# Sequence layer with sparse side path and ternary feed-forward: last head pair and feed-forward part as one instruction program

## The chip, the cores and the metric

The kernel runs on one core of a Trainium2 chip. The metric is the device time of one execution in microseconds; a lower number is better. Times of a timeline are counted from the first instruction of the profiled execution. PE is TensorE, DVE is VectorE, ACT is ScalarE, POOL is GpSimd, SP is SyncE, which here only issues DMAs.

## The reference

One layer over 1024 tokens of width 256, all in fp32. The attention is multi-head with 16 heads, compressed queries and keys (layer-normed), rotary position parts, a causal softmax, and a small side path over 8 selected tokens, which adds one row per head. What the change touches is the second half:

```python
def ternary_quant(w):
    scale = jnp.mean(jnp.abs(w)) + EPS
    q = jnp.clip(jnp.round(w / scale), -1.0, 1.0) * scale
    return w + jax.lax.stop_gradient(q - w)

x = layernorm(x + attention(x))                 # x: (1, 1024, 256)
up   = x @ ternary_quant(W_up).T                # W_up, W_gate: (1024, 256)
gate = x @ ternary_quant(W_gate).T
y = (silu(up) * gate) @ ternary_quant(W_down).T # W_down: (256, 1024)
out = layernorm(x + y)
```

## The kernel before

**Steps and slots.** The heads are worked on in 8 pairs. A list of steps (`PROLOGUE`, `FIRST`, `MID` in a loop, `LAST`, `EPILOGUE`) is written out by hand, and each engine runs the part of each step that belongs to it, in the order of the list. So a step's place in the list is its place in the queue of every engine that takes part in it. A head has 8 slots, one per tile of 128 queries. In slot i: `qk` (five matmuls per chunk of 512 keys into `SC[i % 2]`, line 618 on), DVE's mask with maximum (L1006), ACT's exp (L845) into `Pb[i % 2]`, then `tc`: PE transposes the probabilities (L636), ACT copies them out rounded (`PTh`, L832), DVE subtracts to get the rest (`PTl`, L943). Every fp32 operand goes through PE as such a pair of high and low parts (fp32r). `pv` (L610 to L612) multiplies with the values for 256 queries at a time, `wo` multiplies with the output weights and adds into `acc` (L1143). The last chunks of a head (`tc` of tile 7, `wo` 2, `pv` 3, `wo` 3) stand in the first slots of the next one. The four single PSUM banks `J` go round over all steps that use one; the two double banks `SC` belong to `qk`.

**The last pair** (heads 14 and 15, `LAST`) has no next pair to prepare; the steps of `mlp_steps` (line 277) are in its slots instead. `wld` loads the three weight matrices of the feed-forward part (1 MB each) into `kvraw`, `KX` and `QX`, `wabs` (ACT, L866) sums absolute values, `wtot` turns them into scale and thresholds (a small matmul, and five tiny DVE operations), `tern` makes the ternary values of 512 columns with two DVE operations (L1080: is it below the negative threshold; L1082: is it above the positive one, minus the first), twelve times, in place. `wt` transposes 512 columns of the result on PE (L771) and ACT copies them into `xTh`, `xTl` (up, gate) and `KNh`, `KNl` (down), twelve times. `rowadd` adds the side path's row (L1132), `ln1` and `ln1n` are the layer norm for 256 tokens, `ht` transposes their normed values (L775) and splits them.

**The feed-forward part** is a second block, `mlp` (from line 1165), which starts when all engines have ended the first. It norms and transposes tokens 512 to 1023 itself. Its unit is 512 tokens times 128 hidden columns, 16 of them: `up_gate` (8 matmuls of 512 columns, L1241, L1242), the sigmoid (ACT, L1288), two products (DVE `tt` L1344, `hid` L1349), the rounded copy (ACT `Hh`, L1276), the rest (POOL `Hl`, L1218), and three units later `down` (8 matmuls of 256 columns, L1253, L1254), which accumulates over 8 units in the four banks `J`. After units 7 and 15: residual for four token tiles (L1312), statistics (L1318), POOL's power of -0.5, the norm (L1329), and the store. The second accumulation waits for the first four residuals.

```python
pe.wait_ge(hl_done, n + 1)
if n == ET:
    pe.wait_ge(y_done, 4)
```

## Time and profile before

| what | us |
|---|---|
| median of 3 runs | 739.39 (738.97 to 739.4) |
| the profiled execution, its own time | 743.51 |
| its span, first to last instruction | 741.7 |
| PE busy | 670.4 (90%) |
| DVE busy | 490.9 (66%) |
| ACT busy | 397.5 (54%) |
| POOL busy | 338.9 (46%) |

The page gives busy times over the whole span. A share there is a mean over parts with different limits, so the stretches around the change have to be read apart: the windows give busy time per engine between two moments, and the timeline gives each instruction with, in brackets, the idle time of its engine ahead of it and what ended that. Head 14 begins with its first mask at 600.60, head 15 at 633.78; the first matmul of the feed-forward block is at 682.17.

### The profile page before, as it was taken

The page shows a single profiled execution, that of the slowest core. Times are in us where ns is not written, and L with a number is a line of the kernel's source. Part 1 is how long each engine was busy: PE and PEld are TensorE (multiplying, and loading weights), DVE is VectorE, ACT ScalarE, POOL GpSimd, SP SyncE. Part 2 cuts the span into 40 slices and gives each one's busy share as a digit, 9 for nine tenths or more (in the row PEclk, how much of TensorE's full clock was granted, in tenths as well). Part 3 has the DMA queues.
Part 4 walks back from the last instruction along what each step waited for, and adds up shares of the span by engine and source line. Part 5 has one row for each costly group of instructions (what it writes and reads, how often), then busy time and mean ns, then how long its engine had stood idle before and what let it go on. Part 6 is the DMA issues. An engine that isn't in the chain of part 4 may idle for free. (4 is left out here: it accounts for less than half of the span.)

```text
span 741.7 us, 14057 instructions
## 1 busy us (share of the span) xinstructions
PE 670.4 (90%) x4416; PEld 600.9 (81%) x4416; DVE 490.9 (66%) x1401; ACT 397.5 (54%) x920; POOL 338.9 (46%) x279
## 2 busy tenths in 40 slices
PE   5667799999999999999999999999999999878994
PEld 5546699889988898899889988998899889767883
DVE  2665366666676666666766676667666668996665
ACT  3341345764576457645764476447644766644531
POOL 5622354735474547354735474547454730000443
PEclk9965599999999999999999999999999999998998
DMA  6153210551045105510541055105410545000001
GB/s 200 44 141 72 64 50 1 124 112 51 1 103 134 50 0 120 113 50 0 125 108 50 0 127 106 50 0 129 104 50 0 127 86 171 1 0 1 1 1 57
DMA packets 29486, 50.50 MB, mean 68 GB/s; under 512 B 8976, under 2 KB 20496, under 8 KB 29456
## 3 DMA queue, kind: packets, MB, share of 16 engines
q1 hardware_dynamic: 29456, 50.12, 27.0%
q8 instruction: 16, 0.26, 0.1%
q14 instruction: 14, 0.11, 0.1%
HBM read 15.50 MB, written 1.05 MB: 22 GB/s over the span
## 5 line engine op out<-in xcount | busy, mean ns | idle before, releaser
L943 DVE TENSOR_TENSOR PTl<-J,PTh 128x512 fp32r<-128x512 f32 (+1 forms) x192 | 102.2, 553 | 65.3 <-ACT PTh L832 64.7
L845 ACT ACTIVATE Pb<-SC,nm 128x128 f32<-128x128 f32 (+7 forms) x128 | 94.8, 740 | 62.9 <-DVE nm L1010 62.9
L1006 DVE CUSTOM_DVE_ANT_0 SC<-SC,mask 128x128 f32<-128x128 f32 (+7 forms) x128 | 97.3, 760 | 28.0 <-PE SC L627 25.8
L610 PE MATMUL J<-PTh,Vh 128*128 128x256 f32 x320 | 88.3, 276 | 7.0 <-DVE PTl L943 6.8
L636 PE MATMUL J<-ident,Pb 128*128 128x128 f32 x576 | 88.1, 279 | 6.0 <-ACT Pb L845 5.5
L612 PE MATMUL J<-PTh,Vl 128*128 128x256 f32 x320 | 89.3, 279 | 0.0
L611 PE MATMUL J<-PTl,Vh 128*128 128x256 f32 x320 | 89.3, 279 | 0.0
L832 ACT ACTIVATE PTh<-J 128x512 fp32r<-128x512 f32 (+1 forms) x192 | 87.5, 493 | 2.6 <-PE J L636 1.7
L636 PEld LDWEIGHTS J<-ident,Pb 128*128 128x128 f32 x576 | 63.8, 141 | 13.8 <-ACT Pb L845 5.4
L610 PEld LDWEIGHTS J<-PTh,Vh 128*128 128x128 f32 x320 | 60.7, 190 | 11.7 <-DVE PTl L943 10.4
L623 PE MATMUL SC<-KNh,QNh 128*128 128x512 f32 (+1 forms) x192 | 69.0, 360 | 0.0
L624 PE MATMUL SC<-KNl,QNh 128*128 128x512 f32 (+1 forms) x192 | 66.8, 348 | 0.0
L625 PE MATMUL SC<-KNh,QNl 128*128 128x512 f32 (+1 forms) x192 | 66.8, 348 | 0.0
L626 PE MATMUL SC<-KD,QS 128*128 128x512 f32 (+1 forms) x192 | 66.7, 347 | 0.0
L627 PE MATMUL SC<-KL,QS 128*128 128x512 f32 (+1 forms) x192 | 66.6, 347 | 0.0
L832 ACT ACTIVATE ATh<-J 128x256 fp32r<-128x256 f32 x64 | 24.5, 383 | 69.6 <-PE J L612 68.9
L611 PEld LDWEIGHTS J<-PTl,Vh 128*128 128x128 f32 x320 | 60.6, 189 | 0.7
L612 PEld LDWEIGHTS J<-PTh,Vl 128*128 128x128 f32 x320 | 60.9, 190 | 0.0
L1143 DVE SCALAR_TENSOR_TENSOR acc<-J,rs,acc 128x256 f32<-128x256 f32 x128 | 56.1, 480 | 2.6
L943 DVE TENSOR_TENSOR ATl<-J,ATh 128x256 fp32r<-128x256 f32 x64 | 27.0, 422 | 45.1 <-ACT ATh L832 45.0
L907 ACT ACTIVATE kvraw<-kvraw,nmr,rstd 128x128 f32<-128x128 f32 x128 | 52.5, 485 | 5.0 <-POOL nmr L589 5.0
L832 ACT ACTIVATE kvraw<-J 128x512 f32<-128x512 f32 x32 | 19.2, 599 | 65.8 <-PE J L612 65.8
(283 smaller groups left out, 1869.9 us busy)
## 6 DMA issues: line engine op xcount, KB each, us to landing
KD<-RKh SPq DMA_DIRECT2D x32, 256.0 KB, 4.5
KL<-RKl SPq DMA_DIRECT2D x32, 256.0 KB, 5.0
KX<-KX SPq DMA_DIRECT2D x16, 256.0 KB, 2.4
QX<-QX SPq DMA_DIRECT2D x16, 256.0 KB, 2.3
QS<-RQh SPq DMA_DIRECT2D x16, 256.0 KB, 4.0
QS<-RQl SPq DMA_DIRECT2D x16, 256.0 KB, 4.5
r_kv<-in_L_attn_W_ckv SPq DMA_DIRECT2D x8, 384.0 KB, 3.4
r_qn<-in_L_attn_W_qT SPq DMA_DIRECT2D x16, 128.0 KB, 2.8
```

The costliest lines, as they stand in the source:

```text
L610: mm(o, lhsT=wh, rhs=xh, start=start, stop=False)
L611: mm(o, lhsT=wh, rhs=xl, start=False, stop=False)
L612: return mm(o, lhsT=wl, rhs=xh, start=False, stop=stop)
L623: mm(o[:, k], lhsT=QNh[b][:, q], rhs=KNh[b][:, k], start=True, stop=False)
L624: mm(o[:, k], lhsT=QNh[b][:, q], rhs=KNl[b][:, k], start=False, stop=False)
L625: mm(o[:, k], lhsT=QNl[b][:, q], rhs=KNh[b][:, k], start=False, stop=False)
L626: mm(o[:, k], lhsT=QS[b][:, q], rhs=KD[b][:, k], start=False, stop=False)
L636: last = pe.transpose(o[:, tile(j - 4 * c)], Pb[i % 2][:, tile(j)], ident[:, :])
L832: return act.activation(o, i, ACT.Copy)
L845: act.activation(Pb[i % 2][:, w], SC[i % 2][:, w], ACT.Exp, bias=nm[:, i % 2:i % 2 + 1], scale=SCALE, accum_out=sm[:, b, i:i + 1]).then_in ...
L943: dve.tensor_tensor(o, i, h.bitcast(F32), ALU.subtract).then_inc(done[kind], 1)
L1006: dve.tensor_tensor_reduce(out=SC[i % 2][:, w], in0=SC[i % 2][:, w], in1=mask[:, 128 * (7 - i):S], scale=1.0, scalar=LOW, op0=ALU.add, op1 ...
```

## The change

- The host hands over the three feed-forward weights transposed. The twelve `wt` steps are gone; `tern` writes its result straight to where the matmuls read it.
- The first operation of `tern`, the compare, moves from DVE to POOL. DVE waits for it, and POOL waits for the combine two pieces back.
- Two of the three weights are loaded at the start of head 14 (ahead of the transfers `stk` and `stq` in SP's queue), the third in slot 3. Sums, scales and eight of the twelve `tern` steps lie in head 14, four in head 15; the row additions move from slots 3 and 4 of head 15 to 0 and 1.
- The second block is gone. Its work becomes steps of the list: `ug` (up and gate), `m` (sigmoid, products, copy, rest), `dn` (down), `h2` (late transposes), `res`, `ost`, `onorm`. They stand in `EPILOGUE`, mixed with the last chunks of head 15 and the layer norms of the later tokens. The buffers lie in memory that the attention no longer needs.
- The unit is 256 tokens times 128 hidden columns, 32 of them. Four halves of `SC` banks hold four units, `down` comes five units later, and two accumulators of `J` alternate with the other two.

```diff
                 if b == 0:
-                    add(2, True, ("wld", 0, 0))
-                    add(4, True, ("wld", 0, 1), ("wabs", 0, 0))
-                    add(5, True, ("wabs", 0, 1))
-                    add(6, True, ("wtot", 0, 0), ("wld", 0, 2), ("tern", 0, 0), ("wabs", 0, 2))
-                    add(7, True, ("tern", 0, 1), ("wabs", 0, 3))
+                    add(0, True, ("wld", 0, 0), ("wld", 0, 1))
+                    add(1, True, ("wabs", 0, 0))
+                    add(2, True, ("wabs", 0, 1))
+                    add(3, True, ("wtot", 0, 0), ("wld", 0, 2), ("wabs", 0, 2))
+                    add(4, True, ("wabs", 0, 3), ("tern", 0, 0), ("tern", 0, 1))
+                    add(5, True, ("wtot", 0, 1), ("tern", 0, 2), ("tern", 0, 3))
+                    add(6, True, ("tern", 0, 4), ("tern", 0, 5), ("wabs", 0, 4))
+                    add(7, True, ("tern", 0, 6), ("tern", 0, 7), ("wabs", 0, 5))
                 else:
-                    add(0, True, ("wtot", 0, 1), ("tern", 0, 2))
-                    add(1, True, ("tern", 0, 3), ("wabs", 0, 4))
-                    add(2, True, ("wt", 0, 0), ("tern", 0, 4), ("wabs", 0, 5))
-                    add(3, True, ("rowadd", 0, 0), ("rowadd", 0, 1), ("wt", 0, 1), ("wt", 0, 2), ("tern", 0, 5), ("tern", 0, 6))
-                    add(4, True, ("wtot", 0, 2), ("wt", 0, 3), ("tern", 0, 7), ("rowadd", 0, 2), ("rowadd", 0, 3))
-                    add(5, True, ("wt", 0, 4), ("tern", 0, 8), ("ln1", 0, 0))
-                    add(6, True, ("wt", 0, 5), ("tern", 0, 9), ("ln1n", 0, 0), ("ln1", 0, 1))
-                    add(7, True, ("wt", 0, 6), ("wt", 0, 7), ("tern", 0, 10), ("tern", 0, 11), ("ln1n", 0, 1))
+                    add(0, True, ("wtot", 0, 2), ("rowadd", 0, 0), ("rowadd", 0, 1))
+                    add(1, True, ("rowadd", 0, 2), ("rowadd", 0, 3), ("tern", 0, 8))
+                    add(2, True, ("tern", 0, 9))
+                    add(3, True, ("tern", 0, 10))
+                    add(4, True, ("tern", 0, 11))
+                    add(5, True, ("ln1", 0, 0))
+                    add(6, True, ("ln1n", 0, 0), ("ln1", 0, 1))
+                    add(7, True, ("ht", 0, 0), ("ln1n", 0, 1))
...
-        EPILOGUE = [*t(NH - 1, 7), ("ht", 0, 0), ("wo", NH - 1, 2), ("wt", 0, 8), ("wt", 0, 9), ("pv", NH - 1, 3),
-                    ("ht", 0, 1), ("wt", 0, 10), ("wt", 0, 11), ("wo", NH - 1, 3)]
+        def one(kind, n):
+            return (kind, 0, n)
+
+        def mlp_steps_of(n):
+
+            a = [one("ug", n), one("m", n - 2)]
+            q, e = divmod(n - LAG, ET)
+            if n >= LAG:
+                a.append(one("dn", n - LAG))
+            a += {7: [one("h2", 2)], 9: [one("h2", 3)]}.get(n, [])
+            if q >= 1:
+                a += {1: [one("res", q - 1)], 2: [one("ost", q - 1)], 4: [one("onorm", q - 1)]}.get(e, [])
+            return a
+
+        EPILOGUE = [one("ug", 0), one("ug", 1), *t(NH - 1, 7), ("wo", NH - 1, 2), one("ht", 1), ("pv", NH - 1, 3), one("m", 0),
+                    one("ln1", 2), one("ug", 2), one("ug", 3), one("m", 1), ("wo", NH - 1, 3), one("ln1n", 2), one("ug", 4),
+                    one("m", 2), one("ln1", 3), one("ug", 5), one("m", 3), one("dn", 0), one("ug", 6), one("ln1n", 3),
+                    one("m", 4), one("dn", 1)]
+        for n in range(7, NM):
+            EPILOGUE += mlp_steps_of(n)
...
+        EPILOGUE += [one("m", NM - 2), one("onorm", 2), one("m", NM - 1)] + [one("dn", n) for n in range(NM - LAG, NM)]
+        EPILOGUE += [one("res", 3), one("ost", 3), one("onorm", 3)]
 
...
                     if kind == "wld":
-                        src = (W_up, W_gate, W_down)[c]
-                        if c == 0:
+                        src = (W_upT, W_gateT, W_downT)[c].rearrange("(k p) n -> p k n", p=128)
+                        if c == 2:
                             sp.wait_ge(ready["kt"], PER["kt"] * NH)
                             sp.wait_ge(done["vs"], NH)
                         else:
-                            sp.wait_ge((rk_ready, rq_ready)[c - 1], NP)
-                        sp.dma_start(raw[c], src.rearrange("(t p) d -> p t d", p=128)).then_inc(ld_mlp[c], 16)
+                            sp.wait_ge((rk_ready, rq_ready)[c], NP)
+                        sp.dma_start(raw[c].rearrange("p (k n) -> p k n", n=src.shape[2]), src).then_inc(ld_mlp[c], 16)
+                    if kind == "onorm":
+                        sp.wait_ge(y_ln, c + 1)
+                        sp.dma_start(out[256 * c:256 * c + 256, :].rearrange("(t p) d -> p t d", p=128),
+                                     yo[:, 2 * c:2 * c + 2, :]).then_inc(stored, 16)
...
+                    if kind == "tern":
+                        w, j = c // 4, c % 4
+                        if j == 0:
+                            gp.wait_ge(thr_ready, w + 1)
+                        wait(gp, tern_done, c - 1)
+                        gp.tensor_scalar(low[c % 2], raw[w][:, half(j)], nthr[:, w:w + 1], None, ALU.is_lt).then_inc(low_done, 1)
+                    if kind == "m":
+                        gp.wait_ge(hh_done, c + 1)
+                        gp.tensor_tensor(Hl[c % HB], hid[c % 4], Hh[c % HB].bitcast(F32), ALU.subtract).then_inc(hl_done, 1)
+                    if kind == "ost":
+                        q = slice(2 * c, 2 * c + 2)
+                        inv_std(mv2[:, q, 1], ve2[:, q], rsd2[:, q], y_ag, c + 1, y_ve, y_rsd, c + 1)
...
+            def up_gate(n):
+                wait(pe, hid_done, n - 3)
+                if n % ET == 0:
+                    if n < 2 * ET:
+                        pe.wait_ge(done["ht"], n // ET + 1)
+                    else:
+                        pe.wait_ge(done["h2"], n // ET - 1)
+                if n == 0:
+                    pe.wait_ge(tern_done, 8)
+                if n % 4 < 2 and n < 4:
+                    pe.wait_ge(exp_done, T * NH - 1)
+                elif n < 4:
+                    pe.wait_ge(exp_done, T * NH)
+                tok = slice(256 * (n // ET), 256 * (n // ET) + 256)
+                o = SC[n % 4 // 2]
+                for w in range(2):
+                    z = slice(512 * (n % 2) + 256 * w, 512 * (n % 2) + 256 * w + 256)
+                    for k in range(K):
+                        wt = (xTh, xTl)[w][:, k, tile(n % ET)]
+                        mm(o[:, z], lhsT=wt, rhs=hTh[k][:, tok], start=k == 0, stop=False)
+                        last = mm(o[:, z], lhsT=wt, rhs=hTl[k][:, tok], start=False, stop=k == K - 1)
+                last.then_inc(ug_ready, 1)
+
...
+            def down(n):
+                q, e = divmod(n, ET)
+                pe.wait_ge(hl_done, n + 1)
+                if n == 0:
+                    pe.wait_ge(tern_done, 12)
+                    pe.wait_ge(done["wo"], PER["wo"] * NH)
+                if n == ET:
+                    pe.wait_ge(done["h2"], 2)
+                if e == 0 and q >= 2:
+                    pe.wait_ge(y_done, 2 * q - 2)
+                wt = (KNh, KNl)[e // 4][0][:, D * (e % 4):D * (e % 4) + D]
+                for t in range(2):
+                    o = J[2 * (q % 2) + t]
+                    mm(o[:, 0:D], lhsT=Hh[n % HB][:, tile(t)], rhs=wt, start=e == 0, stop=False)
+                    last = mm(o[:, 0:D], lhsT=Hl[n % HB][:, tile(t)], rhs=wt, start=False, stop=e == ET - 1)
+                last.then_inc(dn_ready, 1)
+
+            def late_transposes(c):
+                pe.wait_ge(ln_done, c + 1)
+                pe.wait_ge(done["wo"], PER["wo"] * NH)
+                for m in range(4):
+                    last = pe.transpose(J[c][:, tile(m)], acc[:, 2 * c + m % 2, tile(m // 2)], ident[:, :])
+                last.then_inc(ready["h2"], 1)
+
             def run(steps, p, before):
...
+            def hidden_hi(n):
+                act.wait_ge(hid_done, n + 1)
+                wait(act, dn_ready, n - HB + 1)
+                copy(Hh[n % HB], hid[n % 4]).then_inc(hh_done, 1)
...
+                    if kind == "m":
+                        act.wait_ge(ug_ready, c + 1)
+                        wait(act, tt_done, c - 3)
+                        act.activation(sg[c % 4], up_of(c), ACT.Sigmoid, scale=scl[:, 0:1]).then_inc(sg_done, 1)
+                        if c >= 1:
+                            hidden_hi(c - 1)
+                        if c == NM - 1:
+                            hidden_hi(c)
...
                     if kind == "tern":
                         w, j = c // 4, c % 4
-                        if w == 2:
-                            v, lw = raw[2][:, j // 2, half(j % 2)], low[c % 2]
-                        else:
-                            v, lw = raw[w][:, 2 * j:2 * j + 2, :], low[c % 2].rearrange("p (t d) -> p t d", t=2)
+                        v, lw = raw[w][:, half(j)], low[c % 2]
+                        dst = (xTh, xTl)[w][:, j // 2, half(j % 2)] if w < 2 else (KNh, KNl)[j // 2][0][:, half(j % 2)]
                         if j == 0:
                             dve.wait_ge(thr_ready, w + 1)
-                        if c == 0:
-                            dve.wait_ge(rq_ready, NP)
-                        if c >= 2:
-                            dve.wait_ge(tern_done, c - 1)
-                        dve.tensor_scalar(lw, v, nthr[:, w:w + 1], None, ALU.is_lt).then_inc(low_done, 1)
                         dve.wait_ge(low_done, c + 1)
-                        dve.scalar_tensor_tensor(v, v, thr[:, w:w + 1], lw, ALU.is_gt, ALU.subtract).then_inc(tern_done, 1)
+                        dve.scalar_tensor_tensor(dst, v, thr[:, w:w + 1], lw, ALU.is_gt, ALU.subtract).then_inc(tern_done, 1)
+                    if kind == "m":
+                        dve.wait_ge(sg_done, c + 1)
+                        dve.scalar_tensor_tensor(tt[c % 4], up_of(c), scl[:, 0:1], sg[c % 4], ALU.mult, ALU.mult).then_inc(tt_done, 1)
+                        dve.wait_ge(tt_done, c + 1)
+                        wait(dve, hl_done, c - 3)
+                        dve.scalar_tensor_tensor(hid[c % 4], gate_of(c), scl[:, 1:2], tt[c % 4], ALU.mult, ALU.mult).then_inc(hid_done, 1)
+                    if kind == "res":
+                        dve.wait_ge(dn_ready, ET * (c + 1))
+                        for t in range(2):
+                            dve.scalar_tensor_tensor(yo[:, 2 * c + t, :], J[2 * (c % 2) + t][:, 0:D], scl[:, 2:3], acc[:, 2 * c + t, :],
+                                                     ALU.mult, ALU.add).then_inc(y_done, 1)
+                    if kind == "ost":
+                        for t in range(2 * c, 2 * c + 2):
+                            dve.wait_ge(y_done, t + 1)
+                            dve.bn_stats(st2[:, t, :], yo[:, t, :]).then_inc(y_st, 1)
+                        for t in range(2 * c, 2 * c + 2):
+                            dve.wait_ge(y_st, t + 1)
+                            ins = dve.bn_aggr(mv2[:, t, :], st2[:, t, :])
+                        ins.then_inc(y_ag, 1)
+                    if kind == "onorm":
+                        dve.wait_ge(y_rsd, c + 1)
+                        dve.wait_ge(y_ag, c + 1)
+                        for t in range(2 * c, 2 * c + 2):
+                            ins = dve.tensor_scalar(yo[:, t, :], yo[:, t, :], mv2[:, t, 0:1], rsd2[:, t:t + 1], ALU.subtract,
```

## Rows read from the trace of the kernel before

**Rows 1.** The page: busy time and share by engine, granted TensorE clock by slice.
```profile
PE 670.4 (90%) x4416; PEld 600.9 (81%) x4416; DVE 490.9 (66%) x1401; ACT 397.5 (54%) x920; POOL 338.9 (46%) x279
...
PEclk9965599999999999999999999999999999998998
```

**Rows 2.** Windows: start:end length, busy PE PEld DVE ACT POOL, clock, DMA, GB/s.
```profile
600.60:633.78 33.18, 31.25 (x221) 28.38 (x220) 25.27 (x68) 23.89 (x56) 3.42 (x2) 1.00 0.41 122
601.00:613.00 12.00, 11.18 (x82) 9.93 (x81) 7.87 (x24) 8.54 (x24) 3.42 (x2) 1.00 0.34 68
612.00:633.78 21.78, 20.67 (x143) 18.86 (x142) 18.00 (x46) 15.15 (x33) 0.00 (x0) 1.00 0.43 146
633.78:665.79 32.01, 27.25 (x191) 24.09 (x190) 30.47 (x87) 15.77 (x38) 0.91 (x2) 1.00 0.00 1
665.79:732.86 67.07, 58.70 (x336) 50.77 (x336) 43.77 (x92) 29.46 (x53) 23.93 (x22) 0.95 0.03 9
732.86:741.70 8.84, 0.00 (x0) 0.00 (x0) 4.73 (x16) 0.00 (x0) 1.21 (x2) 0.61 0.17 59
```

**Rows 3.** Timeline of DVE and ACT in heads 14 and 15: start us, us, instruction.
```profile
627.76 0.48 DVE L1080 TENSOR_SCALAR CS<-kvraw,nthr 128x512 f32<-128x512 f32 x1
628.28 0.75 DVE L1082 SCALAR_TENSOR_TENSOR kvraw<-kvraw,thr,CS 128x512 f32<-128x512 f32 x1
...
650.38 0.79 ACT L845 ACTIVATE Pb<-SC,nm 128x640 f32<-128x640 f32 x1 [2.93 <-DVE nm L1010]
...
653.80 1.29 DVE L1132 TENSOR_TENSOR acc<-acc,row 128x512 f32<-128x512 f32 x2
```

**Rows 4.** Timeline of PE from the last mask to the second half of the feed-forward part.
```profile
667.66 0.66 PE L771 MATMUL J<-ident,KX 128*128 128x128 f32 x4 [2.00 <-DVE ATl L943]
...
676.79 0.28 PE L610 MATMUL J<-PTh,Vh 128*128 128x256 f32 x1
...
682.17 0.47 PE L1241 MATMUL SC<-QNh,xTh 128*128 128x512 f32 x1 [1.52 <-PEq L1156]
...
715.75 0.36 PE L1253 MATMUL J<-KNh,Hh 128*128 128x256 f32 x1 [1.24 <-DVE yo L1312]
```

**Rows 5.** Windows of 5 us around the hand-over, columns as in rows 2.
```profile
650.00:655.00 5.00, 3.13 (x24) 2.87 (x25) 4.71 (x16) 2.35 (x5) 0.00 (x0) 1.00 0.00 0
665.00:670.00 5.00, 2.41 (x19) 1.72 (x17) 4.17 (x12) 3.23 (x7) 0.89 (x2) 0.99 0.00 0
670.00:675.00 5.00, 4.33 (x21) 4.04 (x20) 4.85 (x12) 2.21 (x5) 0.00 (x0) 0.50 0.02 3
```

**Rows 6.** Timeline of PE in the steady ring of the feed-forward part.
```profile
695.82 0.40 PE L1241 MATMUL SC<-QNh,xTh 128*128 128x512 f32 x1
...
697.64 0.28 PE L1253 MATMUL J<-KNh,Hh 128*128 128x256 f32 x1
...
698.58 0.40 PE L1241 MATMUL SC<-QNh,xTh 128*128 128x512 f32 x1
```

**Rows 7.** Groups by line (busy, mean ns, idle before), one line's instructions, SP's timeline.
```profile
L576 POOL CAST Vh<-kvraw 128x1024 fp32r<-128x1024 f32 x16 | 16.7, 1041 | 80.3 <-ACT kvraw L907 80.3
...
L1218 POOL TENSOR_TENSOR Hl<-hid,Hh 128x512 fp32r<-128x512 f32 x16 | 20.7, 1291 | 24.3 <-ACT Hh L1276 24.3
...
L548 POOL TENSOR_TENSOR Wqnl<-r_qn,Wqnh 128x256 fp32r<-128x256 f32 x16 | 11.8, 737 | 1.3
...
L1143 DVE SCALAR_TENSOR_TENSOR acc<-J,rs,acc x128: 472/480/486, 101.6 to 681.4; 128x256 f32<-128x256 f32 x128
...
L1288 ACT ACT_TABLE_LOAD x1 | 1.3, 1283 | 1.4 <-PEq L1156 1.4
...
588.04 0.46 SPq L426 DMA_DIRECT2D QS<-RQh  x1
```

**Rows 8.** Timeline of DVE after the last matmul.
```profile
732.86 1.66 DVE L1312 SCALAR_TENSOR_TENSOR yo<-J,scl,acc 128x256 f32<-128x256 f32 x4 [3.32 <-PE J L1254]
...
737.64 1.38 DVE L1329 TENSOR_SCALAR yo<-yo,mv,rsd 128x256 f32<-128x256 f32 x4 [1.40 <-POOL rsd L1226]
```

More of the change, by code:

```diff
@@ L41 @@
 NB = 4
+ET = E // 128
+NM = 4 * ET
+LAG = 5
 CHUNKS = [(i + 4) // 4 for i in range(T)]
@@ L145, in attention_and_mlp, with ring, up_of, gate_of @@
         low = [CS[:, 0, 512 * c:512 * c + 512] for c in range(2)]
-        raw = [kvraw[:, :, :], KX[:, :, :].rearrange("p k n -> p (k n)").rearrange("p (t d) -> p t d", t=T), QX[:, :, :]]
+        raw = [X[:, :, :].rearrange("p k n -> p (k n)") for X in (KX, QX, kvraw)]
         junk = CS[:, 1, :]
+        def ring(X, n=4):
+            return [X[:, 256 * i:256 * i + 256] for i in range(n)]
+        HB = 8
+        hTh, hTl = (QNh[0], QNl[0]), (QS[0], KD[0])
+        Hh, Hl = ring(RKh) + ring(RKl), ring(RQh) + ring(RQl)
+        sg, tt, hid = ring(QX[:, 0, :]), ring(QX[:, 1, :]), ring(CS[:, 0, :])
+        yo = KX[:, :, :].rearrange("p k n -> p (k n)").rearrange("p (t d) -> p t d", t=T)
+        def up_of(n):
+            return SC[n % 4 // 2][:, 512 * (n % 2):512 * (n % 2) + 256]
+        def gate_of(n):
+            return SC[n % 4 // 2][:, 512 * (n % 2) + 256:512 * (n % 2) + 512]
+        st2, mv2 = sb("st2", [128, T, 6]), sb("mv2", [128, T, 2])
+        ve2, rsd2 = sb("ve2", [128, T]), sb("rsd2", [128, T])
         mx = sb("mx", [128, 2])
@@ L243, in attention_and_mlp @@
         PER = {"xt": 4, "qc": T, "qm": 4, "kv": 4, "kpe": 2, "qp": 2, "kt": 2, "ab": 1, "qn": 2,
-               "vs": 1, "pv": 4, "wo": 4, "side": 11, "tc": NCH, "wb": 1, "rw": 1, "wtot": 3, "wt": 12, "ht": 2}
+               "vs": 1, "pv": 4, "wo": 4, "side": 11, "tc": NCH, "wb": 1, "rw": 1, "wtot": 3, "ht": 2}
         def count(kind, unit, c):
@@ L496, in _ @@
             run(LAST, NP - 1)
+            run(EPILOGUE, 0)
+            sp.wait_ge(stored, 64)
         LD_C, LD_SIDE, LD_W0 = 16 * 8, 16 * 8, 16 * 7
@@ L762, in use @@
                     last = mm(o[:, 0:2], lhsT=onesf[:, :], rhs=asum[:, 2 * c:2 * c + 2], start=True, stop=True)
-                if kind == "wt":
-                    w, q = c // 4, c % 4
-                    pe.wait_ge(tern_done, 4 * (w + 1))
-                    for m in range(4):
-                        if w < 2:
-                            src = raw[w][:, 4 * (q % 2) + m, tile(q // 2)]
-                        else:
-                            src = raw[w][:, m % 2, tile(2 * q + m // 2)]
-                        last = pe.transpose(o[:, tile(m)], src, ident[:, :])
                 if kind == "ht":
@@ L796, in run @@
                         qk(unit(kind, off, p), p + off // 2, off % 2, c)
+                    elif kind == "ug":
+                        up_gate(c)
+                    elif kind == "dn":
+                        down(c)
+                    elif kind == "h2":
+                        late_transposes(c)
                     elif kind in BANKED_ALL:
@@ L846, in run @@
                                        scale=SCALE, accum_out=sm[:, b, i:i + 1]).then_inc(exp_done, 1)
-                    if kind in ready and kind not in ("side", "wb", "wtot", "wo", "rw"):
+                    if kind in ready and kind not in ("side", "wb", "wtot", "wo", "rw", "h2"):
                         act.wait_ge(ready[kind], count(kind, u, c))
```

227 lines of the change are left out of this document (27 added, 200 removed).

## The prediction

> **What bounds the kernel now.** I read the page first: TensorE (PE) is busy 90% of the span and VectorE (DVE) 66%, and the granted clock is full in most slices, with dips near the end [rows 1]. Then I cut the part that the change touches into stretches [rows 2] and looked for the engine with no idle time in each. Head 14 (the first of the last pair) takes 33.18 us with PE busy for 31.25: PE sets its pace. From the first mask of head 15 at 633.78 to its last one at 665.79 the picture turns round: 32.01 us, DVE busy 30.47, PE only 27.25. The DVE timeline shows why: each ternary piece is a compare (0.48) and a combine (0.75), started 0.51 and 0.67 apart, 1.18 us for the two, and ten of the twelve pieces lie in head 15, with four row additions (0.6 each) [rows 3] and half of the first layer norm. The third stretch, 67.07 us from there to the last matmul at 732.86, has 8.4 us of idle PE. The PE timeline shows where some of it sits: 2.00 us ahead of a weight transpose, 1.52 at the start of the second block (released by a queue, not by data), 1.24 in the middle of the feed-forward part while the residual empties the four accumulators [rows 4]. PE was busy 2.41 us in 665 to 670, and the granted clock was 0.50 in the next five [rows 5]; that is 1.2 GHz. Last comes a tail without any matmul, 8.84 us. In the feed-forward ring itself PE has no gap: eight matmuls of 512 columns take 1.82 us (695.82 to 697.64), eight of 256 take 0.94 (to 698.58) [rows 6].
>
> **The change, stretch 1: the ternary work (600.60 to 665.79, 65.19 us).** Leaves DVE: 12 compares. Moves from head 15 to head 14: combines 2 to 7 and the second set of scale steps (0.7). In head 15, DVE loses eight pieces of 1.18 (2 to 9) and 0.7, and keeps four combines of 0.67 ahead of the last mask: 9.4 + 0.7 - 2.7 = 7.4 us less, which gives a floor of 32.0 - 7.4 = 24.6. PE loses 28 transposes of the weights there (0.11 each, 3.1) and has some 22 us of its own up to that mask. With both engines near 90% neither runs without gaps; head 14, where PE had 31.25 of 33.18 and DVE 25.27, shows gaps of 2 us at that load [rows 2]. I take 26.5, 5.5 less than before. Head 14: DVE gains eight combines (5.4) and one more set of scale steps (0.7) and loses two pieces (2.4), 3.7 us, against 3.8 us idle from 612.00 to 633.78; ScalarE gains two more absolute sums (1.1 each) in slots 1 and 2, against 3.5 us idle from 601.00 to 613.00 [rows 2]. The cover is all used up, so I charge 1.0; the bounds are 0 and +3. Stretch 1 is 4.5 us shorter.
>
> The compares go to GpSimd, which is busy for 3.4 us of head 14 and 0.9 of the rest [rows 2]. None of its rows is a compare with a scalar; the nearest are the cast (1041 ns for 1024 columns, so 0.6 for 512) and the two-input subtraction (1291 for 512) [rows 7]. Either is hidden: two are needed per slot of about 4 us, and DVE's combine of piece c waits for one issued a slot before. If one took over 2 us, DVE would stand behind it with its masks, and ScalarE's exps behind those. GpSimd's compares queue behind nothing but the value split of head 15, its only work in head 14 (3.4 us). Loads: the first two now come earlier, behind the last stacking transfer of head 14 at 588.04 [rows 7], and ahead of head 15's stacking, which is wanted only at 633; the four transfers that follow them on SP wait a few us at most, at no cost. The third is wanted in slot 6. Host-side transposition isn't in the device time.
>
> **Stretch 2: hand-over and feed-forward (665.79 to 732.86, 67.07 us).** PE's work after the change: 256 up/gate matmuls of 256 columns at 0.1175 (30.1; before 128 of 512 at 0.228, 29.1), 128 down matmuls (15.0), 16 transposes of the normed tokens in `ht` and `h2` (1.8), and what is left of head 15: 15 transposes 1.7, `pv` 2.1 and 2.8, `wo` 1.4. Sum 54.9. Now the idle time, counted from the last mask M. DVE's mask 1.4, then exp, `pv`'s eviction, `ht` 0's copies and subtractions: `ug` 0 can start at about M+6.0, while PE's own work ends at M+3.4: idle 2.6. The transposes of tile 7 then `wo`, `ht` 1; `pv` 3 waits 0.6 for its subtraction and ends at M+13.4. ScalarE reaches the first sigmoid only behind `pv` 3's copy, and behind a table load of 1283 ns [rows 7]: M+15.1. From there DVE is the bound: each step `m` is two products. A product of 256 columns with one PSUM input takes 480 ns [rows 7], 0.39 from start to start (four of them in 1.66) [rows 8], so a step costs 0.91, and between the first ones lie `wo` 3 (1.0) and two layer norms (1.6 each). PE waits for the fourth `hid` before: 6.3 us idle in all up to `ug` 10 at M+27.9, the 2.6 and 0.6 included. After that a step costs PE 0.94 + 0.47 = 1.41, DVE 0.91, GpSimd 0.74 (256-column subtraction, 737 ns) [rows 7] and ScalarE 0.7, so PE is the bound again; residual and norm of a quarter cost DVE 2.6 per eight steps against 4.0 spare, and use other accumulators than the next quarter, so the 1.24 us goes. At the end the last `ug`'s chain (sigmoid, two products, copy, subtraction, 3.6 with `onorm` 2 between) outlasts the downs in hand: 1.3 idle, and 0.5 I give to small gaps. 54.9 + 6.3 + 1.3 + 0.5 = 63.0, 4.1 less. So nearly all of this gain is work (2.2 of 20 weight transposes, 3.3 that matmuls lose at half clock, from 670.1 to 676.8, where the 256-column matmul is back at 0.28 [rows 4, 5]), and the idle time moves rather than shrinks. Bounds: 60 (DVE's extra steps overlap better) and 66 (they don't overlap, and the clock falls again).
>
> ScalarE's switch of tables: the row shows 1283 ns, with 1.4 us idle ahead of it put down to the block's start [rows 7]. If that idle is the switch's own, it now stands in the stream, and the first sigmoid comes 1.4 later. The Trainium skill, ScalarE: Activation LUTs, section What ACT_TABLE_LOAD costs, says the switch is a load of about 1283 ns and a drain of about 1380 ns; the row agrees on the load and can't tell for the drain; by that rule the sum would be 1.4 higher.
>
> **Stretch 3: the tail (8.84 us).** Before: four residuals from 732.86, statistics, GpSimd's power, four normalisations from 737.64 [rows 8], and 2.7 from the end of these to the end of the span. Now only two tiles are left: 0.9 + 0.8 + 0.35 for residual, statistics and their sum, 0.1 of hand-over, 0.9 on GpSimd, 0.8 for the norm, 2.7 for the store: 6.6, 2.2 less.
>
> Sum: 4.5 + 4.1 + 2.2 = 10.8 us. The profiled execution took 743.51 with a span of 741.7, so its own time would be 732.7. The median of the runs is 739.39, 4.1 below the profiled one, and the cut is the same: **728.6**.
>
> **The rivals.** (a) The table switch costs the full 2.7 in the stream: 730.0. For: the idle time of just that size; against: every engine waited then. (b) The clock falls once more, as in [rows 5], through PE's wait ahead of `ug` 0; 6.7 us at 1.2 GHz cost 3.3: 731.9. Against: 3.13 busy of five at 650 to 655 left it full, and the new stretch has about that. (c) Head 15 doesn't get shorter, since what sets it is the round mask, exp, transpose, subtraction, `pv`, and DVE was only full beside it: 728.6 + 5.5 = 734.1. For: DVE's load was spread over gaps; against: an exp waited 2.93 us for its mask there [rows 3]. It is also the case where the spreading does nothing. (d) Slower: GpSimd's compares hold up DVE. No compare in the trace ran on GpSimd beside a DVE operation with two SBUF inputs, which the combines and row additions have. If DVE stood still for each compare, 12 x 1.29 = 15.5 us on the stretches where it is the bound: 744.1. It decides from 0.9 us per compare on. Against: the subtraction on GpSimd takes 1291 ns on average beside DVE's products in the ring. The Trainium skill, GPSIMD Engine Reference, section 8. Key points, says that GpSimd shares its SBUF interfaces with VectorE and contends with instructions in a 2-port mode or with two SBUF inputs; no run here shows it yet. (e) Slower too: half clock stays through the feed-forward part, where PE waits for DVE in the first steps. A step then costs 2.8 and not 1.41; eight such steps eat the gain, fourteen give 748.
>
> **How the numbers follow.** Chances: forecast 0.46, (a) 0.14, (b) 0.17, (c) 0.13, (d) 0.06, (e) 0.04. The likeliest is the forecast, 728.6. The range: downward, stretch 1 at its floors (2.9 less) and a fill with 2 us less idle: 724; upward past (c) with a part of (a): 736. (d) and (e) are left out, and with misses at both ends that is about 0.2. A measurement of this kernel tells 0.2% (1.5 us) from no change. Faster 0.89; same 0.04 (half of (d), and chance sums of (b) and (c)); slower 0.07.
>
> **What would show it.** Stretch 1: from head 15's first mask to its last about 26.5 us, DVE busy under 95%; head 14 about 34. Compares on GpSimd of 0.6 to 1.3 us each, combines still 0.75. Stretch 2: 63 us from last mask to last matmul, PE idle ahead of `ug` 0 and from `ug` 4 to `ug` 9, none of over 0.3 after that; first sigmoid 1.7 after the end of `pv` 3. Stretch 3: 6.6. Wrong if combines are longer beside compares, if the granted clock is 0.5 past the hand-over, or if head 15 keeps its 32 us with DVE idle.

## The result, and the profile after

| | before | changed kernel |
|---|---|---|
| median, us (first comparison, 6 runs each) | 739.39 (738.97 to 742.97) | 734.7 (731.98 to 736.2) |
| ratio | | 0.9925 [0.9898, 0.9953] |
| median, us (second comparison, 9 and 5 runs) | 740.83 (739.51 to 742.04) | 734.32 (732.39 to 736.45) |
| ratio | | 0.9905 [0.9889, 0.9921] |
| profiled execution, own time / span, us | 743.51 / 741.7 | 736.02 / 734.2 |

The change makes the kernel faster, by 0.75% and 0.95% (4.7 and 6.5 us). The forecast was 728.6: the sign is right, and 734.7 lies in the range of 724.0 to 736.0, but the forecast gain was 10.8 us, and about half of it came.

The page after the change: busy time by engine, and the granted clock by slice [rows 1].

```profile
PE 667.7 (91%) x4496; PEld 604.6 (82%) x4496; DVE 491.5 (67%) x1421; ACT 397.2 (54%) x940; POOL 365.4 (50%) x313
...
PEclk9875599999999999999999999999999999999998
```

The totals say little: nearly the same work, with POOL busy 26.5 us longer. The windows of the stretches of [rows 2] tell more. First head 14, from its first mask; then head 15 to its last mask; the hand-over and the feed-forward part up to the last residual pair; the tail; and three windows of 5 us at the hand-over, which answer [rows 5]. The columns are length, busy PE, PEld, DVE, ACT, POOL, clock, DMA share and GB/s.

```profile
601.18:637.10 35.92, 32.67 (x224) 28.76 (x223) 28.44 (x78) 25.99 (x60) 17.08 (x10) 1.00 0.26 65
637.10:662.43 25.33, 22.35 (x154) 20.14 (x152) 23.85 (x70) 9.80 (x26) 9.05 (x6) 1.00 0.00 1
662.43:727.99 65.56, 57.55 (x453) 55.31 (x452) 50.35 (x127) 33.43 (x81) 29.10 (x44) 0.97 0.04 13
727.99:734.20 6.21, 0.00 (x0) 0.00 (x0) 2.49 (x8) 0.00 (x0) 0.89 (x2) 0.59 0.13 42
...
660.00:665.00 5.00, 3.86 (x32) 3.54 (x30) 4.72 (x13) 2.11 (x5) 0.89 (x2) 1.00 0.00 0
665.00:670.00 5.00, 3.08 (x17) 3.08 (x18) 1.95 (x5) 1.08 (x5) 0.00 (x0) 0.77 0.00 0
670.00:675.00 5.00, 4.65 (x35) 4.44 (x34) 2.90 (x7) 1.85 (x4) 0.00 (x0) 0.89 0.01 3
```

| stretch | before | forecast | after |
|---|---|---|---|
| head 14 | 33.18 | 34.2 | 35.92 |
| head 15 to its last mask | 32.01 | 26.5 | 25.33 |
| last mask to last matmul | 67.07 | 63.0 | 65.56 |
| tail | 8.84 | 6.6 | 6.21 |
| sum from the start of head 14 | 141.1 | 130.3 | 133.0 |

Head 15 gave more than forecast, head 14 cost more, and the stretch at the hand-over kept most of what it was to lose. Its 65.56 us hold 57.55 of PE busy and 8.0 of PE idle. The idle time is the 8.1 that the forecast had (2.6, 3.7 more in the first steps, 1.3 and 0.5); the busy time is 2.6 above the 54.9. The clock column shows a part of it: 0.77, then 0.89. PE's timeline shows the waits and the slower matmuls.

```profile
666.92 0.39 PE L867 MATMUL SC<-QNh,xTh 128*128 128x256 f32 x1 [3.06 <-DVE KD L1238]
667.14 0.28 PE L868 MATMUL SC<-QS,xTh 128*128 128x256 f32 x1
...
668.39 0.41 PE L868 MATMUL SC<-QS,xTh 128*128 128x256 f32 x1
668.61 0.41 PE L867 MATMUL SC<-QNl,xTh 128*128 128x256 f32 x1
...
679.38 0.39 PE L867 MATMUL SC<-QNh,xTh 128*128 128x256 f32 x1 [0.64 <-DVE CS L1197]
681.21 0.38 PE L867 MATMUL SC<-QNh,xTh 128*128 128x256 f32 x1 [0.62 <-DVE CS L1197]
683.86 0.39 PE L867 MATMUL SC<-QNh,xTh 128*128 128x256 f32 x1 [0.78 <-DVE CS L1197]
688.16 0.39 PE L867 MATMUL SC<-QNh,xTh 128*128 128x256 f32 x1 [0.33 <-DVE CS L1197]
...
727.21 0.39 PE L884 MATMUL J<-KNl,RKl 128*128 128x256 f32 x1 [1.90 <-POOL RQl L641]
```

The first `ug` waits 3.06 us for the subtraction of `ht` 0 (L1238), as forecast. Less than a microsecond later the matmuls of 256 columns follow each other every 0.21 us instead of 0.12, which is the lower level, 1.2 GHz. Then `ug` waits for DVE's second product (L1197) four times, 2.4 us in all, and never again by over 0.3. At the end the last `down` waits 1.90 us for GpSimd.

Two later runs, `e2_short_sums` and `e7_short_combines`, have this same stretch with no edit in it, and in both the clock stays full. Here is the stretch in `e2_short_sums`, and the 5 us up to where the clock fell in the changed kernel with the 3.4 us after it:

```profile
661.19:725.35 64.16, 55.99 (x453) 53.76 (x452) 50.36 (x128) 33.32 (x81) 29.11 (x44) 1.00 0.04 14
...
661.46:666.46 5.00, 1.93 (x17) 1.70 (x16) 4.05 (x10) 3.08 (x7) 0.88 (x2) 1.00 0.00 0
666.46:669.86 3.40, 3.40 (x30) 3.18 (x28) 0.91 (x2) 1.09 (x2) 0.00 (x0) 1.00 0.00 0
```

and the last two in the changed kernel:

```profile
662.70:667.70 5.00, 1.94 (x17) 1.70 (x16) 4.05 (x10) 3.08 (x7) 0.88 (x2) 1.00 0.00 0
667.70:671.10 3.40, 3.40 (x18) 3.40 (x17) 0.00 (x0) 0.12 (x1) 0.00 (x0) 0.50 0.00 0
```

The engines had done the same in both up to that moment, PE after a wait of 3.07 and 3.06 us. Then one execution kept the full clock and the other had half of it for 3.4 us. The low level cost the stretch 1.4 us (65.56 against 64.16; 64.18 in `e7_short_combines`). Of the five profiled executions with this order, three had it (also `e1_compare_dve` and `e9_after_again`) and two had not.

### The profile page after: what moved, and what is told of

The parts are those of the page before. It is cut to its first block, busy times and chain, and to the rows that moved or that the text cites. A ratio compares the mean times of both kernels' runs of the same rounds, so it can differ in the third digit from the quotient of the medians.

```text
span 734.2 us, 14324 instructions
## 1 busy us (share of the span) xinstructions
PE 667.7 (91%) x4496; PEld 604.6 (82%) x4496; DVE 491.5 (67%) x1421; ACT 397.2 (54%) x940; POOL 365.4 (50%) x313
## 3 DMA queue, kind: packets, MB, share of 16 engines
HBM read 15.50 MB, written 1.05 MB: 23 GB/s over the span
## 4 chain that ended last, share of the span: by engine, by line
PE 57%; DVE 16%; ACT 11%; issue 9%; POOL 4%; SPq 1%; DMA 0%; ACTq 0%; DVEq 0%; POOLq 0%
PE J L676 10%; PE J L678 9%; PE J L677 9%; DVE PTl L1059 4%; PE J L702 4%; ACT kvraw L1023 3%; PE SC L693 3%; PE SC L690 3%; PE SC L691 3%; PE SC L692 3%; ACT Pb L960 3%; PE SC L689 3%; POOL rstd L608 3%; DVE SC L1122 3%; ACT PTh L942 2%
## 5 line engine op out<-in xcount | busy, mean ns | idle before, releaser
L630 POOL CAST Vh<-kvraw 128x1024 fp32r<-128x1024 f32 x16 | 16.6, 1037 | 81.0 <-ACT kvraw L1023 81.0
```

## The experiments

Each edit is against the changed kernel. Stretches are those of the table.

**The compares back on DVE** (`e1_compare_dve`).

```diff
 # GpSimd
-if kind == "tern": ...
-    gp.tensor_scalar(low[c % 2], raw[w][:, half(j)], nthr[:, w:w + 1], None, ALU.is_lt)...
 # DVE, ahead of the combine
+wait(dve, tern_done, c - 1)
+dve.tensor_scalar(lw, v, nthr[:, w:w + 1], None, ALU.is_lt).then_inc(low_done, 1)
```

> The changed kernel with the 12 compares of the ternary work back on DVE, nothing else. Theory (the move to GpSimd is what shortens DVE's queue): DVE gets 12 x 0.51 = 6.1 us more in a stretch where it is busy 22 of 24.5 us (head 14 from its fourth mask) and 23.9 of 25.3 (head 15), so head 14 goes from 35.9 to about 38 and head 15 up to its last mask from 25.3 to about 27.3; 4 to 5 us longer than the changed kernel, ratio to the kernel before about 0.999. Rival (DVE and GpSimd hinder each other, since the compares take 1.6 to 2.6 us on GpSimd and one combine beside one took 1.10 in place of 0.74): the move bought little, both heads within 0.5 us of the changed kernel, ratio about 0.993.

Measured: 742.51 us, 1.0022 [1.0001, 1.0042] of before. Its windows for head 14 and for head 15:

```profile
601.49:641.60 40.11, 33.94 (x226) 29.87 (x225) 32.35 (x86) 26.16 (x60) 3.41 (x2) 0.98 0.22 58
641.60:669.49 27.89, 24.23 (x155) 21.58 (x155) 25.27 (x75) 9.80 (x26) 0.91 (x2) 0.91 0.00 1
```

With the compares on DVE, stretch 1 is 68.0 us against 61.25, and longer than before (65.19). So the spreading over both heads alone brings nothing; the move to GpSimd is worth 6.8 us, more than the 4 to 5 expected. Eight compares of 0.51 are 4.1 of the 4.2 us by which head 14 grew: each of its last four slots holds two compares and is 1.04 to 1.05 us longer, the first three of them ahead of any low clock. In head 15 four compares are 2.0 of 2.6, and there the clock is also lower (0.91). DVE's idle time in head 14 covers none of these compares.

**The absolute sums over 8 columns** (`e2_short_sums`).

```diff
-src, o = raw[w][:, S * j:S * j + S], junk
+src, o = raw[w][:, S * j:S * j + 8], junk[:, 0:8]
```

> The changed kernel, but each of the six absolute sums on ScalarE reads 8 columns, not 1024, so its scale is of 8 columns only (work left out). Theory (head 14 took 2.7 us longer because two more sums stand in ScalarE's queue in slots 1 to 4, ahead of copies and exps that PE waits for): each sum falls from 1.15 us to 0.3 and head 14 from 35.9 to 33.5 to 34. Rival (it is DVE's eight combines and scale steps): head 14 stays at 35.3 or more.

Measured: head 14 35.09 us, 0.83 shorter; head 15 the same (25.35); 733.37 us in one run. That lies between the theory (33.5 to 34) and the rival (35.3 or more). ScalarE's busy time in head 14 is 21.36 us instead of 25.99: 4.6 us less of its work give 0.8, so most of the growth is not ScalarE's. Single profiles can carry such a difference: in five executions with the changed kernel's head 14 and a full clock it took 35.82 to 35.96 us.

**The first part alone** (`e3_pair_only`): the changed last pair, then the old second block.

```diff
-EPILOGUE = [one("ug", 0), one("ug", 1), *t(NH - 1, 7), ...]   # ug, m, dn, h2, res, ost, onorm
+EPILOGUE = [*t(NH - 1, 7), ("wo", NH - 1, 2), ("ht", 0, 1), ("pv", NH - 1, 3), ("wo", NH - 1, 3)]
...
+mlp(nc, top, SC, J, acc, ident, mhalf, epst, ...)   # as before, 512 tokens at a time
```

> First part of the change alone: weights from the host in transposed form, ternary work spread and shared as in the changed kernel, but the feed-forward part as in the kernel before (own block, 512 tokens at a time). If the parts add up as the windows say, the last pair gives 3.9 us up to the last mask, the 20 weight transposes behind it 2.2, and the clock falls or not as PE idles there (0 to 3): 5 to 8 us less than before in the profile, and the second part is then worth about nothing in its long stretch and 2.6 in the tail: ratio 0.990 to 0.994. Rival (the second part carries most of the gain, by the block boundary and the tail): ratio above 0.996.

Measured: 735.63 us, 0.9933 [0.9903, 0.9963]. Its windows from the last mask to the first matmul of the block, and from there to the last residuals:

```profile
659.88:672.68 12.80, 7.76 (x62) 6.83 (x61) 8.60 (x24) 5.17 (x13) 0.89 (x2) 1.00 0.00 0
672.68:723.33 50.65, 48.09 (x264) 41.21 (x264) 32.88 (x64) 21.82 (x37) 23.07 (x20) 0.97 0.03 12
```

The first part gives nearly the whole gain. Without the weight transposes, and with the clock full where it was 0.50 before [rows 5], the hand-over takes 12.80 us (16.38 before); the block takes 50.65 (50.69 before). One program with units of 256 tokens is then 2.1 us longer (65.56 against 63.45) in this stretch and 2.7 shorter in the tail (6.21 against 8.87), in the profiles from head 14 on 0.4 us shorter in sum (133.0 against 133.4). Both profiles hold 3.4 us of low clock in this stretch.

**Tile 7 ahead of the first two up/gate groups** (`e4_tile7_first`).

```diff
-EPILOGUE = [one("ug", 0), one("ug", 1), *t(NH - 1, 7), ("wo", NH - 1, 2), one("ht", 1), ...
+EPILOGUE = [*t(NH - 1, 7), ("wo", NH - 1, 2), one("ug", 0), one("ug", 1), one("ht", 1), ...
```

> The changed kernel with the transposes of the last query tile and wo 2 ahead of the first two ug steps in the list (they stand behind them in the changed kernel). Theory (the 3.06 us in which PE waits for the split of the normed tokens, with the clock falling after it, is a matter of order: tile 7 is ready at 665.1): PE fills 1.6 us of the wait, pv 3 starts 3 to 4 us earlier, the clock stays full; 2.5 to 4 us less than the changed kernel, ratio to before about 0.988. Rival (the fill afterwards is set by DVE's products and norms, so an earlier pv 3 is eaten up by it): less than 1 us.

Measured: 730.82 us, 0.9893 [0.9844, 0.9941]. The window of the stretch:

```profile
659.92:721.73 61.81, 55.77 (x453) 53.71 (x452) 50.38 (x128) 33.23 (x81) 29.12 (x44) 1.00 0.04 14
```

and, from PE's timeline, the gap ahead of the tile-7 transposes and the first of the four waits for products:

```profile
662.78 1.06 PE L702 MATMUL J<-ident,Pb 128*128 128x128 f32 x8 [1.44 <-ACT Pb L960]
...
673.12 0.39 PE L867 MATMUL SC<-QNh,xTh 128*128 128x256 f32 x1 [0.64 <-DVE CS L1197]
```

PE now waits 1.44 us for the last exp and has the transposes of tile 7 to do while `ht` 0 is prepared. The clock stays full. The stretch is 3.75 us shorter than the changed kernel's 65.56: 1.4 is the low clock, and 2.35 is the order itself (61.81 against the 64.16 with the old order at full clock), nearly all of it idle time that is gone.

**The first products earlier too** (`e5_products_early`): `pv` 3 behind two products, and the later norms spread.

```diff
+EPILOGUE = [*t(NH - 1, 7), ("wo", NH - 1, 2), one("ug", 0), one("ug", 1), one("m", 0), one("ht", 1), one("m", 1),
+            ("pv", NH - 1, 3), one("ug", 2), one("ln1", 2), one("ug", 3), one("m", 2), ("wo", NH - 1, 3), one("ug", 4),
+            one("ln1n", 2), one("m", 3), one("ug", 5), one("dn", 0), one("ln1", 3), one("m", 4), ...
```

> e4_tile7_first with the first two m steps (sigmoid, products, copy, rest) ahead of pv 3 in the list, and the norms of the late tokens a step or two later. Theory (from last mask to last matmul what is left of idle PE, 0.64, 0.62, 0.78 and 0.33 ahead of ug 4 to ug 8, is DVE's products coming in a heap behind pv 3 while ACT and DVE idle for 2 us and more ahead of it): that stretch falls from 61.8 us in e4 to 59 to 60; ratio to before about 0.986. Rival (the products delay the subtraction that pv 3 waits for, and PE's work of 55 us plus the end of the chain is all there is): within 0.7 us of e4.

Measured: 727.96 us, 0.9827 [0.9791, 0.9863]. The window of the stretch:

```profile
660.99:719.33 58.34, 54.54 (x453) 53.45 (x452) 50.42 (x128) 33.73 (x81) 29.20 (x44) 1.00 0.05 15
```

and all of PE's waits of over 0.2 us from the last mask to the steady ring:

```profile
663.85 1.06 PE L702 MATMUL J<-ident,Pb 128*128 128x128 f32 x8 [1.45 <-ACT Pb L960]
...
680.92 0.38 PE L867 MATMUL SC<-QNh,xTh 128*128 128x256 f32 x1 [0.27 <-DVE CS L1197]
```

3.5 us less again, more than expected. The four waits for DVE's products came from the order of the list, not from DVE's load. The busy time falls too, though the 453 matmuls are the same and the clock is full in both: after a wait a first matmul stands 0.22 us ahead of the next instead of 0.12, and the last one before a wait shows its whole 0.28. So busy time also holds some 0.3 us for each wait (an estimate from 55.99 with nine gaps in PE's timeline in `e2_short_sums` and 54.54 with four here).

**The table loaded earlier** (`e6_load_early`): `e4_tile7_first` with a sigmoid of one column behind `wo` 2.

```diff
+if kind == "warm":
+    act.activation(junk[:, 0:1], nm[:, 0:1], ACT.Sigmoid)
```

> e4_tile7_first with a sigmoid of one column on ACT behind wo 2, so that the table load of 1.28 us falls into ACT's idle time and the first real sigmoid finds its table; the list is else as in e4. Theory (the load is on the path of the fill): last mask to last matmul 60.5 us, 1.3 less than e4. Rival (PE's 55 us of work hides it, since ug 2, ug 3 and wo 3 run meanwhile): 61.3 or more.

Measured: stretch 60.39 us against 61.81, 731.54 in one run. ScalarE's timeline around the load in the changed kernel:

```profile
676.12 0.38 ACT L942 ACTIVATE ATh<-J 128x256 fp32r<-128x256 f32 x1 [2.73 <-PE J L678]
676.52 1.28 ACT L989 ACT_TABLE_LOAD   x1
677.81 0.84 ACT L989 ACTIVATE QX<-SC,scl 128x256 f32<-128x256 f32 x2
```

and in this one:

```profile
666.66 1.09 ACT L942 ACTIVATE PTh<-J 128x512 fp32r<-128x512 f32 x2
667.77 1.28 ACT L987 ACT_TABLE_LOAD   x1
669.06 0.20 ACT L987 ACTIVATE CS<-nm 128x1 f32<-128x1 f32 x1
```

In both the load starts 0.02 us after the last copy ended (at 676.50 and 667.75), and the next operation stands 0.01 behind its end. So the switch costs its 1.28 us and nothing beside it, and all of that was on the path: loading early gained 1.4 in the stretch. The one run's total isn't below the 730.82 of `e4_tile7_first`; in its profile head 14 starts at 601.86 instead of 598.64, behind unchanged code.

**The combines over 8 of 512 columns** (`e7_short_combines`).

```diff
-dve.scalar_tensor_tensor(dst, v, thr[:, w:w + 1], lw, ALU.is_gt, ALU.subtract)
+dve.scalar_tensor_tensor(dst[:, 0:8], v[:, 0:8], thr[:, w:w + 1], lw[:, 0:8], ALU.is_gt, ALU.subtract)
```

> The changed kernel, with each of DVE's twelve combines on 8 of 512 columns (work left out: the rest of the ternary weights isn't written). Compares on GpSimd stay whole. Theory (DVE's added work is what lengthens head 14 beyond 33.2, and e2_short_sums leaves 35.1 of the 35.9): eight combines of 0.67 fall to about 0.1, head 14 to 33.5 to 34.5, and head 15 up to the last mask from 25.3 to about 23.5. Rival (what counts is the wait for GpSimd's compares, which stays): head 14 at 35.3 or more.

Measured: head 14 34.12 us (1.8 shorter, with DVE busy for 24.73 instead of 28.44), head 15 24.63 (0.7 shorter, where 1.8 was expected), 730.73 in one run. GpSimd's timeline of the compares in the changed kernel (start, then the time of all that stand in a row, x2 or x3):

```profile
617.47 3.12 POOL L638 TENSOR_SCALAR CS<-KX,nthr 128x512 f32<-128x512 f32 x2 [5.05 <-DVE nthr L1183]
621.66 3.54 POOL L638 TENSOR_SCALAR CS<-KX,nthr 128x512 f32<-128x512 f32 x2 [1.06 <-DVE xTh L1191]
...
640.60 6.57 POOL L638 TENSOR_SCALAR CS<-kvraw,nthr 128x512 f32<-128x512 f32 x3 [5.38 <-DVE nthr L1183]
```

and with the short combines:

```profile
616.09 3.13 POOL L638 TENSOR_SCALAR CS<-KX,nthr 128x512 f32<-128x512 f32 x2 [5.06 <-DVE nthr L1183]
619.75 3.10 POOL L638 TENSOR_SCALAR CS<-KX,nthr 128x512 f32<-128x512 f32 x2 [0.54 <-DVE xTh L1191]
```

A compare takes 1.56 us with no full combine or row addition beside it; beside a full combine it takes about 2.0, and the three at 640.60 take 6.57, the first two of them (2.46 and 2.60) beside row additions. With short combines all eight of head 14 take 1.56, while those beside the row additions of head 15 still take 2.46 and 2.59.

**Both lists changed** (`e8_both`): `e5_products_early`, with head 14's feed-forward steps in other slots.

```diff
-add(0, ("wld", 0, 0), ("wld", 0, 1)); add(1, ("wabs", 0, 0)); add(2, ("wabs", 0, 1)); add(3, ("wtot", 0, 0), ...)
+add(0, ("wld", 0, 0), ("wld", 0, 1), ("wabs", 0, 0), ("wabs", 0, 1)); add(2, ("wtot", 0, 0)); add(3, ..., ("tern", 0, 0))
```

> e5_products_early, with two absolute sums in slot 0 of head 14 (ACT idle there for 2.4 us) in place of 1 and 2, and the first scale steps and the first ternary piece a slot earlier. Theory (sums and DVE's load in slots 1 to 5 cost head 14 its 2.7 us): head 14 falls from 35.9 to about 34.8, the rest as e5; ratio to before 0.983 to 0.986. Rival (DVE's total load sets it, whatever the slot): head 14 stays within 0.4 of 35.9.

Measured: 728.11 us, 0.9818 [0.979, 0.9847]; head 14 34.90 (1.0 shorter than in `e5_products_early`), the hand-over 58.80 (0.5 longer; there the clock fell during the last matmuls, and the window has 0.99). So the slots matter in head 14, with all the work in place, as the theory had it. In the whole the gain doesn't show: the median can't be told from `e5_products_early` alone.

**The changed kernel and the early order once more, on one chip** (`e9_after_again`, `e10_early_again`), neither with a new edit.

> The changed kernel once more, unaltered, in more runs and on the chip of the next one, because its gain was half of the forecast and part of the gap (2.8 us) was put down to the two profiled executions not lying at the same distance from their medians. If that is so, the median stays near 735 and the ratio to the kernel before near 0.992, and the profiled own times of further executions lie between 732 and 736. If instead the first six runs were drawn low or high, the ratio moves: the sum of the stretches measured from the start of head 14 on (133.0 against 141.1) would give 8.1 us, a ratio of 0.989.

> The order with the products early (tile 7 of pv 2 ahead of the first two up/gate groups, pv 3 behind two products) on the same chip as the unaltered changed kernel. The stretches say 125.9 against 133.0 from the start of head 14 on, 7.1 us: 1.0% below the changed kernel of the same batch. If most of that gain were the chip of the earlier batch, it comes out under 0.5% below.

Measured: 734.32 us and 0.9905 [0.9889, 0.9921] for the changed kernel, 726.63 us and 0.9801 [0.9784, 0.9819] for the early order, 1.0% below it. The profiled execution of `e9_after_again` had head 14 at 37.28 us (35.92 in the first one), with the rest alike (25.36, 65.58, 6.28). The 5 us ahead of the fall of the clock in its head 14, and the 3.4 us with the low level:

```profile
608.80:613.80 5.00, 4.03 (x25) 3.00 (x24) 3.70 (x10) 4.94 (x12) 2.56 (x2) 1.00 0.20 45
613.80:617.20 3.40, 3.40 (x14) 2.98 (x13) 2.26 (x9) 2.21 (x5) 0.70 (x1) 0.50 0.70 240
```

and the two that answer them in the first profile of the changed kernel:

```profile
609.77:614.77 5.00, 4.03 (x25) 3.02 (x24) 3.69 (x10) 4.94 (x12) 2.56 (x2) 1.00 0.21 48
614.77:618.17 3.40, 3.40 (x25) 3.15 (x24) 2.76 (x10) 2.70 (x6) 0.70 (x1) 1.00 0.70 239
```

The same program with the same busy times up to that moment once keeps the full clock and once has half of it for 3.4 us, and head 14 is 1.4 us longer. `e10_early_again` has the same loss (37.27 us); the other five executions with this head 14 have not.

## Why the prediction was right in sign and short in size

**What bounds the kernel.** Right. Head 15 was DVE's: DVE's busy time there fell by 6.6 us (30.47 to 23.85), and the stretch by 6.7 (forecast 5.5, floor 7.4). Rival (c), that head 15 keeps its 32 us, is out, although its 734.1 lies nearest to the result.

**Head 14, the term mis-sized.** Charged 1.0, measured 2.7 (35.92 against 33.18), inside the bounds of 0 and 3. The prediction said the cover was all used up and yet took the low side. The runs say whose work it is: taking out ScalarE's sums gives 0.8 back (`e2_short_sums`), taking out 3.7 us of DVE's combines gives 1.8 (`e7_short_combines`). Both take out more than the change added, so this is a division in the rough. `e8_both` adds that 1.0 of it goes when the same steps stand in other slots.

**The compares.** Forecast 0.6 to 1.3 us, measured 1.56, and 1.9 to 2.6 beside DVE's two-input operations: the nearest rows, a cast and a subtraction, were no bound for it. It cost next to nothing, because the step that hides them held: GpSimd's rows above carry waits for DVE (5.05 and 1.06 us), and no row of DVE carries one for GpSimd's compares. Rival (d) had a real mechanism in the wrong place. Here is where DVE paid: the combines of the last weight, in DVE's timeline.

```profile
640.42 1.28 DVE L1268 TENSOR_TENSOR acc<-acc,row 128x512 f32<-128x512 f32 x2
...
644.20 1.10 DVE L1191 SCALAR_TENSOR_TENSOR KNh<-kvraw,thr,CS 128x512 fp32r<-128x512 f32 x1
...
647.25 0.74 DVE L1191 SCALAR_TENSOR_TENSOR KNh<-kvraw,thr,CS 128x512 fp32r<-128x512 f32 x1
```

One combine of twelve took 1.10 instead of 0.74, and two row additions kept their 1.28 (1.29 before [rows 3]). That combine takes 1.09 to 1.10 in the other profiles of this code too, and 0.75 in `e1_compare_dve`, without compares on GpSimd. With 8 columns it still takes 0.57 where the other eleven take 0.22, so the loss is 0.35 us whatever its length. DVE lost 0.4 us where the rival gave it 15.5; GpSimd's twelve compares took 21.8 us, where 12 x 1.56 is 18.7. The Trainium skill (GPSIMD Engine Reference, section 8. Key points) states that GpSimd contends with VectorE's instructions that have two SBUF inputs. These rows agree, with GpSimd bearing nearly all of it.

**The hand-over, the step that failed.** 65.56 us for 63.0: 1.4 of the 2.6 is the low clock, and the rest is the 64.16 of the same stretch at full clock against 63.0. The step that failed is the choice against rival (b). It argued that 3.13 busy of five had left the clock full at 650 to 655 [rows 5]. In the new stretch PE was busy for 1.94 of the 5 us before the clock fell, and with 1.93 it stayed full in two other executions. So neither the forecast nor the rival could be had from such rows; the record has the low level in three of five, and no run shows what decides it. Rival (b) had the place right; its price of 3.3 was too high, since the low level held for 3.4 us, not 6.7, and cost 1.4.

The sum of PE's work has an error of its own. It counts the 2.1 us of `pv` 2 behind the last mask, and they lie ahead of it:

```profile
660.39 0.28 PE L676 MATMUL J<-PTh,Vh 128*128 128x256 f32 x1
...
662.18 0.22 PE L676 MATMUL J<-PTh,Vh 128*128 128x128 f32 x1
```

These are the first and the last of its six groups of three, and the mask starts at 662.43. The sum stands for 469 matmuls and the window holds 453, two of them the ends of `pv` 2. Without it 54.9 is 52.8. Most of what fills it up again to the 55.99 of `e2_short_sums` is the busy time around waits (2.6 us by the estimate under `e5_products_early`), which the sum leaves out. So PE's own work ended 1.4 us after the start of the last mask and not 3.4, and `ug` 0 started 4.5 us after it, not 6.0; the gap came out near the forecast (3.06 for 2.6) because both ends lay earlier. Of the other idle time the first steps had less than forecast and the end had more (1.9 for 1.3), so that the agreement of 8.0 with 8.1 is in part luck.

**The table switch.** Right: 1.28 us and no more. Rival (a) took the 1.4 us ahead of the load in [rows 7] for a part of the switch; in both rows above the load starts 0.02 us after the last copy. The Trainium skill (ScalarE: Activation LUTs, section What ACT_TABLE_LOAD costs) adds a drain of about 1380 ns to the load's 1283. These traces agree on the load and show no such drain.

**The tail.** 6.21 for 6.6. Its rows (the residuals, POOL's power, the norm) answer [rows 8]:

```profile
727.99 0.88 DVE L1201 SCALAR_TENSOR_TENSOR KX<-J,scl,acc 128x256 f32<-128x256 f32 x2 [2.08 <-PE J L885]
...
730.19 0.69 POOL L608 TENSOR_TENSOR rsd<-ve,mhalf 128x2 f32<-128x2 f32 x1
730.92 0.74 DVE L1215 TENSOR_SCALAR KX<-KX,mv,rsd 128x256 f32<-128x256 f32 x2 [1.18 <-POOL rsd L608]
```

**The cut to the median.** The stretches from head 14 on fell by 8.1 us, the profiled own time by 7.5, the medians by 4.7 and 6.5. The prediction took the 4.1 us between the profiled execution of before and its median as fixed. The changed kernel's profiled executions lie only 1.3 and 2.1 above theirs. So 2.8 of the 6.1 us between 728.6 and 734.7 are this step, the largest single term, and the rest (3.3) is in the profile: head 14 starting 0.6 later behind unchanged code, stretch 1 +0.55, the hand-over +2.6, the tail -0.4. The record shows what the 4.1 was: the 41 timed executions of the kernel before lie between 736.95 and 743.96 us (median 740.82), so the profiled one, 743.51, was near their slow end, and 739.39 was a low median of few runs. Clock losses like the one in head 14 of `e9_after_again` are one source of this spread. The part ahead of head 14 is another: in the eleven profiles of changed kernels head 14 starts between 598.00 and 601.86 us behind the same code. Why it does is open.

**Where the expected gain is.** In the order of the list. The early order takes back 7.2 us of stretch 2 (58.34 against 65.56) with the same instructions, or 5.8 us against the old order at full clock (64.16), and gives 0.9801 of before.

## What to carry to other kernels

When two programs are joined so that one's start fills the other's end, write out for the first steps which engine each waits for. The list of the changed kernel put two `ug` steps that wait for a chain on DVE ahead of transposes that were ready sooner; changing the order alone was worth 5.8 us of the stretch at full clock, and the joining in its first order 0.4. Don't price work put into the "idle" time of an engine at nothing: on DVE it cost half to all of its length (1.8 of 3.7 us for the combines, 4.2 of 4.1 for the compares), on ScalarE about a sixth (0.8 of 4.6). And one profiled execution's distance to its median isn't a constant: time the kernel often enough to see where that execution lies, and carry a few microseconds of it in the range.
